# A macaron layer of two expert blocks around attention: order of the expert weights' loads, of the router's copies, of one normalisation's statistics, and a second area for split shared weights

## The reference

```python
def layernorm(x): return (x - mean(x)) / sqrt(var(x) + 1e-5)

def ffn(x2, gate_w, w_gate_up, w_down, sh_gate_up, sh_down):     # 1024 tokens of 512
    g_s, u_s = split(x2 @ sh_gate_up.T)                          # shared: inner width 512
    shared = silu(g_s) * u_s @ sh_down.T
    probs = softmax(x2 @ gate_w.T)                               # 16 experts
    top_w, top_i = top_k(probs, 2); top_w /= top_w.sum()
    out_e = (silu(x2 @ gate_e.T) * (x2 @ up_e.T)) @ down_e.T     # expert: inner width 128
    return sum(top_w * out_e over the 2 chosen) + shared

x = x + 0.5 * ffn(layernorm(x), ...)
x = x + attention(layernorm(x))        # causal, 2 x 512 tokens, 32 heads on 8 key/value heads of 128
x = x + 0.5 * ffn(layernorm(x), ...)   # same weights again
```

## Time and profile before

| | us |
|---|---|
| median of 3 runs | 1133.6 |
| lowest, highest | 1132.75, 1134.34 |
| the profiled execution's own time | 1136.42 |
| its span in the profile | 1134.4 |
| PE busy | 1092.4 (96%) |
| DVE busy | 798.8 (70%) |
| ACT busy | 640.2 (56%) |
| POOL busy | 541.7 (48%) |

### The profile page before, as it was taken

One profiled execution on the slowest core, in us unless ns is written; L12 is line 12 of the kernel. 1 busy time (PEld: TensorE's weight loads), 2 busy tenths in 40 slices (PEclk: granted clock), 3 DMA queues, 4 the chain that ended last, 5 costly groups with the idle time before them and its releaser, 6 DMA issues.

```text
span 1134.4 us, 22421 instructions
## 1 busy us (share of the span) xinstructions
PE 1092.4 (96%) x6584; PEld 943.7 (83%) x6584; DVE 798.8 (70%) x2139; ACT 640.2 (56%) x1737; POOL 541.7 (48%) x540
## 2 busy tenths in 40 slices
PE   8979999899999999999999999999999998989997
PEld 6867877688988988998898898898899986777875
DVE  7857868766766667667676676666766777668866
ACT  4347753466656556646555665655665655357750
POOL 1545647165337336426526533733642540456644
PEclk9989999999999999999999999999999999999999
DMA  9995665100200200110110020020010005955546
GB/s 355 409 347 189 189 213 191 49 1 1 94 2 1 93 0 0 48 44 0 37 55 0 0 92 0 0 92 0 0 37 1 1 2 191 385 203 168 186 164 208
DMA packets 38622, 114.85 MB, mean 101 GB/s; under 512 B 4384, under 2 KB 4384, under 8 KB 36512
## 3 DMA queue, kind: packets, MB, share of 16 engines
q1 hardware_dynamic: 33440, 97.30, 23.8%
q0 software_dynamic: 5120, 16.78, 4.3%
HBM read 79.20 MB, written 34.87 MB: 101 GB/s over the span
## 4 chain that ended last, share of the span: by engine, by line
PE 80%; DVE 6%; DMA 4%; ACT 4%; POOL 3%; issue 3%; SPq 0%; DVEq 0%; POOLq 0%; ACTq 0%
PE bank L1610 22%; PE bank L1649 13%; PE bank L1741 9%; PE bank L1682 9%; PE bank L1585 7%; PE bank L1623 6%; PE bank L1596 4%; PE bank L1499 2%; PE bank L1546 2%; DMA xn<-x_rows 2%; POOL yg L593 1%; POOL x_rows L582 1%; PE bank L1518 1%; PE bank L1737 1%; PE bank L1678 1%
## 5 line engine op out<-in xcount | busy, mean ns | idle before, releaser
L611 POOL TENSOR_TENSOR scores<-scores,pinv 128x512 f32<-128x512 f32 (+3 forms) x256 | 180.2, 736 | 205.4 <-DVE pinv L1317 205.4
L1216 DVE TENSOR_TENSOR pT_lo<-bank,pT_hi 128x512 fp32r<-128x512 f32 (+2 forms) x192 | 101.0, 554 | 92.9 <-ACT pT_hi L849 92.7
L554 POOL TENSOR_TENSOR tback_lo<-experts,tback_hi 128x768 fp32r<-128x768 f32 x62 | 114.0, 1840 | 65.9 <-ACT tback_hi L756 65.7
L878 ACT ACTIVATE scores<-scores,nmax 128x512 f32<-128x512 f32 (+3 forms) x256 | 140.6, 561 | 0.0
L1281 DVE CUSTOM_DVE_ANT_0 scores<-bank,causal 128x512 f32<-128x512 f32 (+3 forms) x256 | 112.2, 486 | 1.4 <-issue 0.4
L849 ACT ACTIVATE pT_hi<-bank 128x512 fp32r<-128x512 f32 (+2 forms) x192 | 87.0, 489 | 41.6 <-PE bank L1623 41.5
L1610 PE MATMUL bank<-xnT_hi,wqs_hi 128*128 128x512 f32 x256 | 102.8, 402 | 0.6 <-DVE vv_lo L1220 0.6
L1610 PE MATMUL bank<-xnT_lo,wqs_hi 128*128 128x512 f32 x256 | 101.4, 396 | 0.0
L1610 PE MATMUL bank<-xnT_hi,wqs_lo 128*128 128x512 f32 x256 | 101.3, 396 | 0.0
L1623 PE MATMUL bank<-ident,scores 128*128 128x128 f32 x640 | 91.1, 273 | 2.8 <-DVE pT_lo L1216 2.4
L1623 PEld LDWEIGHTS bank<-ident,scores 128*128 128x128 f32 x640 | 75.6, 141 | 11.8 <-DVE pT_lo L1216 2.6
(11 more groups left out here) (242 smaller groups left out, 3516.5 us busy)
## 6 DMA issues: line engine op xcount, KB each, us to landing
experts<-in_ffn_w SPq DMA_DIRECT2D x32, 768.0 KB, 11.4
xn<-x_rows SPq DMA_DIRECT2D x62, 256.0 KB, 2.8
y_rows<-xn SPq DMA_DIRECT2D x62, 256.0 KB, 2.0
raw_q<-in_wq SPq DMA_DIRECT2D x8, 1024.0 KB, 5.4
raw_d<-in_wd SPq DMA_DIRECT2D x8, 1024.0 KB, 4.8
x_rows<-experts SPq DMA_DIRECT2D x1, 7936.0 KB, 30.7
raw_w<-in_ffn_w SPq DMA_DIRECT2D x8, 768.0 KB, 6.5
raw_kv<-in_wkv SPq DMA_DIRECT2D x8, 512.0 KB, 3.5
```

Of the source, the lines that this page charges most:

```text
L554: nc.gpsimd.tensor_tensor(tback[par][1][:], experts[:, bass.ds(at + FRONT, GU - FRONT)], tback[par][0][:].bitcast(F32), ALU.subtract).then ...
L611: nc.gpsimd.tensor_tensor(s, s, pinv[k % 2][:, i:i + 1].to_broadcast([P, P * (i + 1)]), ALU.mult).then_inc(att.normed, 1)
L878: nc.scalar.activation(s, s, ACT.Exp, bias=nmax[par][:, i:i + 1], scale=-1.0, accum_out=psumr[par][:, i:i + 1]).then_inc(att.exp, 1)
L1216: nc.vector.tensor_tensor(pT[1][:, lo_col:hi_col], bank[b][:, 0:hi_col - lo_col], pT[0][:, lo_col:hi_col].bitcast(F32), ALU.subtract).then ...
```

## The change

Four edits go together.

1. **Experts' loads.** The experts come in quarters of four. For `n = 0` only experts 0 to 5 are issued ahead of the scatter's wait (4 and 5 after the first quarter has landed); 6 and 7 follow the loads of tiles 0 to 3; 8 to 11 follow those of tiles 4 and 5 and a wait for the second quarter; 12 follows the store of tile 2 and waits for the third quarter; 13, and 14 with 15, stand between loads and stores of tiles 8 to 10. For `n = 1` experts 4 to 7 wait until the first quarter has landed, 8 to 11 until two have, 12 to 15 until three have. Expert 13 (`HELD_BACK`) waits besides for `u_mm >= 4`, slot 3's up product, in either block. ACT's waits count in quarters, in both blocks, up to step 9; after that all 16 are awaited.
2. **Second pair of areas.** `wgu_odd` holds the odd quarters of the shared gate/up weights. It lies over the experts' area (from 20 x 1024 numbers on, which is in experts 13 and 14); so `cut_gu(3)` waits until all tiles are done. `cut_gu` now stands ahead of `gate` in ACT's list, and `low_gu` ahead of `multiply` in DVE's.
3. **Router.** The first half's logits are copied ahead of `gate(0)`, the second half's behind it; `high(0)` follows. DVE's `low(0)` moves behind the router's first part.
4. **Statistics and adds.** Of `statistics(2, 0)`, the BN_STATS of tiles 2 and 3 move to the end of the slot ahead (`statistics_ahead`), the rest behind the three `turned_lo` of the last slot; the chain of small steps after it (`scaled`) moves into the last slot, and ACT's `roots` behind its last `turned_hi`. In each block's end half of `combine(n, 0)` moves behind `multiply` of slot 6. At the kernel's end `add_down` of slot 7 is divided: two tiles' adds stand ahead of `combine(1, 6)`.

```diff
-EARLY_TILES = 7
-LOADED_HALF = NEXP // 2 * 16
+EARLY_TILES = 9
+QUARTER = NEXP // 4
+LOADED_QUARTER = QUARTER * 16
+LOADED_ALL = NEXP * 16
+WGU_AT = 20 * GU
+HELD_BACK = WGU_AT // FW
...
+        def gate_weights(e):
+
+            return wgu_odd if e % 2 else wgu
+
...
+            quarter = LOADED_QUARTER * (QUARTER - 1)
+            early = [(word >> 4 * (k - 1) if k else word << 4) & quarter for k in range(RING + 2)]
+            return at, [e + LOADED_QUARTER for e in early]
...
                 def load_expert(e):
+                    if e == HELD_BACK:
+
+                        sp.wait_ge(ffn[n].u_mm, 4)
                     sp.dma_start(experts[:, e * FW:(e + 1) * FW], ffn_w[e]).then_inc(moe[n].weights, 16)
...
+                def quarters_there(count):
+
+                    sp.wait_ge(moe[n].weights, count * LOADED_QUARTER)
+
+                def load_quarter(q):
+                    for e in range(QUARTER * q, QUARTER * q + QUARTER):
+                        load_expert(e)
+
+                load_quarter(0)
                 if n == 1:
-                    load_shared(n, 2)
-
-                sp.wait_ge(moe[n].weights, LOADED_HALF)
+                    quarters_there(1)
+                    load_quarter(1)
+                load_shared(n, 2)
                 if n == 0:
...
+                    quarters_there(1)
+                else:
+                    for q in (2, 3):
+                        quarters_there(q)
+                        load_quarter(q)
...
+                def some(experts_at):
+                    if n == 0:
+                        for e in experts_at:
+                            load_expert(e)
...
+                some((4, 5))
                 sp.wait_ge(route[n].scattered, 2 * TT * 16)
                 for k in range(4):
                     load_tile(n, 0, k)
...
+                some((6, 7))
                 load_tile(n, 1, 0)
...
                 load_tile(n, 1, 1)
-                for e in left[3:]:
-                    load_expert(e)
+                if n == 0:
+                    quarters_there(2)
+                some((8, 9, 10, 11))
                 for k in range(4):
                     store_tile(n, 0, k)
                     if k < 2:
                         load_tile(n, 1, k + 2)
-                with sp.Fori(2, TILES // 4) as it:
+                    if n == 0 and k == 2:
+                        sp.wait_ge(once.cleared, 16)
+                        quarters_there(3)
+                        some((12,))
+                for k in range(4):
+                    load_tile(n, 2, k)
+                    some(((13,), (14, 15), (), ())[k])
+                    store_tile(n, 1, k)
...
-                wait(act, f.u_mm, 2 * e)
-                nc.scalar.activation(wgu[0][:].rearrange("p c k i -> p (c k i)"), raw_w[e % 2][:, 0:GU],
+                wait(act, f.u_mm, 2 * (e - 1))
+                if e == NSH - 1:
+
+                    act.wait_ge(moe[n].y_mm, TILES)
+                nc.scalar.activation(gate_weights(e)[0][:].rearrange("p c k i -> p (c k i)"), raw_w[e % 2][:, 0:GU],
...
-                        back(1 - par, at[k + 2], there[k + 2] if n == 0 and j < EARLY_TILES else 2 * LOADED_HALF)
+                        back(1 - par, at[k + 2], there[k + 2] if j < EARLY_TILES else LOADED_ALL)
...
-                shared(n, 0, 1)
-                router(n)
+                router(n, 0)
+                gate(n, 0)
+                router(n, 1)
+                high(n, 0)
...
-                combine(n, 0)
+                combine(n, 0, (0,))
                 multiply(n, SLOTS - 2)
+                combine(n, 0, (1,))
                 low(n, SLOTS - 2)
...
+            add_down(1, SLOTS - 1, range(0, HALF // 2))
             combine(1, 6)
-            add_down(1, SLOTS - 1)
+            add_down(1, SLOTS - 1, range(HALF // 2, HALF))
```

83 lines of the change are left out of this document (42 added, 41 removed).

## The result

| | us |
|---|---|
| changed kernel, median of 10 runs | 1138.26 (1135.23 to 1141.82) |
| kernel before, median of 10 runs on the same chip | 1134.21 (1132.40 to 1138.09) |
| ratio, 95% interval | 1.0031 (1.0016 to 1.0046) |
| changed kernel, span of the profiled execution (its time 1137.25) | 1135.4 |
| PE busy | 1096.7 (97%) |

The change costs 0.3%, some 4 us. Forecast were 1126.5 us and a gain of 7; the result lies outside the range, on the other side.

A forecast was written before the change was run, and what follows sets the result against it. PE, busy 96% of the span, was taken as the bound, so only its waits could gain. -4.9 - 0.3 - 0.7 - 1.15 = -7.05 us from 1133.6 gave 1126.5 us, range 1121.5 to 1130.5.

The forecast's parts named there:

- Step 1, the scatter: First block: with fewer expert loads beside it, the scatter lands at 60.9 for 63.66 us, -2.8 us.
- Step 1, the clock: First block, after the scatter: a shorter PE wait means less loss at half rate, -0.5 us.
- Step 1, tile 6: First block: the tile's load lands at 81.6, before PE asks at 82.1; its wait goes, -1.8 us.
- Step 1, tile 10: First block: the load behind experts 14 and 15 lands within half a us of its need, +0.2 us.
- Rival A: First block: experts queued ahead delay loads of tiles 6, 8 and 10; kernel slower by 3.1 us, 1136.7; chance 0.05.
- Step 2, second areas: Splitting of shared gate/up weights only changes place and hides; price 0, between -0.2 and +1.1 us.
- Step 3, router: Router: earlier first logits copy saves PE's 0.67 us wait; worth -0.66 us ahead of the second block's scatter.
- step 4, end of attention: End of attention: moved statistics remove PE's 2.44 us wait, but later waits take most back; -0.95 us.
- Step 5, the second scatter: Second block: experts 13 to 15 beside the scatter give back 1.6 us; -0.3 us together with router and end of attention.
- The sign that was named for this: Forecast is wrong if SP's waits for quarters leave the DMA engines idle longer than 2 us each.
- rival C: Second block: scatter lands 6.69 us after its last issue and low clock follows, +2 us; 1128.7; chance 0.13.
- Step 6, ends: Block ends: moved multiply gives -0.7 us in the first, two adds moved ahead give -1.15 in the second.

The follow-up runs named there:

- e8: Changed kernel with late experts issued behind tiles' loads in both blocks and stores behind loads; 1135.66 us, 0.9867 of before, where before takes some 1151 us.
- e9: e8 with the first block's loads and stores put back as in the changed kernel; 0.9971 of before, where before takes some 1135 us.
- e11: e8 without the second pair of areas and with no expert held back; 1127.72 us, 0.9929 of before, where before takes some 1135 us.
- e5: The kernel before, unchanged, traced as a control on a chip of the slower kind, where it takes some 1151 to 1152 us.
- e16: Kernel before with only the second pair of areas and the second block's loads by quarters; 1.0057 of before, where before takes some 1135 us.

## Why the prediction was wrong, point by point

**Step 1, the scatter: right, and too small.** Forecast -2.8 us, landed at 60.9; it landed at 58.32, and PE's first tile came 5.3 us earlier. Of the 2.6 us between, 1.6 are the time from last issue to landing, 4.3 us forecast from the second block, 2.72 measured, and 2.7 in e8 and e9 too (994.67 to 997.40; 995.31 to 998.04). The 4.3 were not free of loads, as the step said: SP's loads had ended by some 994, but the scatter's own backlog kept the engines full until 998. The other 1.0 us is the last issue, at 55.59 and not 56.6: POOL started 0.8 us earlier instead of 0.35, and its sixteen pieces took 20.3 us in place of 20.9. The Trainium skill, page "DMA: Bandwidth & Descriptors", section "Anatomy of one DMA — SWDGE (gpsimd) path", gives about 2.0 us of fixed cost and the bytes on top; 2.7 for 256 KB agrees with that.

**Step 1, the clock: -0.5 forecast, no gain measured.** PE's first wait was 0.38 us and not 3.0. But the 1.46 us wait behind it, which was to stay, grew to 1.94, and the half rate came there, until 71.4. From the first tile's row until PE asks for tile 6 it is 19.0 us in both traces.

**Step 1, tile 6: right by luck.** The forecast had the row at 82.1 without a wait; it stands at 81.93 with a wait of 1.82. Two errors cancel. PE asked at 80.1, 2 us earlier than forecast, since the scatter had landed earlier. The load landed at 81.88 for 81.6, 23.6 us behind the scatter's landing instead of 20.7: four experts were to take 7.7 us behind SP's wait, yet from 68.39, when eight had landed, tile 6's load took until 81.9, since tiles' loads and stores run beside (4.5 MB in all, where four experts are 3.15).

**Step 1, tile 10: the failed step.** "+0.2", because the load "lands within half a us of its need". It took 8.22 us, issued 2.4 us behind experts 14 and 15 and not 5; tile 10 waits 2.68 us and ACT 2.21, and the low clock comes with it: +5.6 us between tile 6 and tile 12 where +0.2 stood. Tiles were asked for from PE's side and the queue was a check at the end. From the scatter on it is the queue that sets the time: ten experts stand behind it in place of seven, and from its landing at 58.3 until the last expert's at 96.3 the queue moves 12.7 MB with the DMA engines 92% busy. What PE had won at the first tile became waiting at a later one. Rival A had this mechanism, with waits of 1.8, 3.4 and 5.2 us for the 1.8, 0.3 and 2.7 measured, and got a chance of 0.05. e11 bears it out from the other side: the same early scatter, no wait, and 5.2 us less at the block's last tile than e9.

**Step 2, second areas "price 0".** Right for what it looked at: PE never waited for the split weights on chips at 1135. On chips at 1151 it does, 5.10 us in e5, which the trace of the forecast couldn't show.

**Step 3, router, and step 4, end of attention: right.** Forecast -1.6 ahead of the second scatter; the router's row is 1.7 us earlier, 0.4 of it from the first block, and the 0.67 us wait for the logits behind it is gone too. The 2.08 us wait is the "some 2 us for `left_a_lo`"; the further 1 us ahead of the transposes didn't come, so the end of attention gave 1.3 us for 0.95. The scatter's last issue is 2.7 us earlier instead of 1.6; the granted clock of the router's stretch, which step 5 left open, rose to 1.00.

**Step 5, the second scatter: right mechanism, wrong size, and the second step that failed.** Forecast: last issue 995.35, landed at 1001.6, PE at 1004.2 after 2.7, another 1.0 by the clock, price -0.3 for steps 3 to 5. Measured: 994.22, 1002.67, 1005.19 after 5.84, and 2.3 by the clock. Against before, tile 0's first product is 2.8 us later, though attention began 0.4 us earlier: +3.2 for -0.3. PE was free at 999.4 and not at 1001.5, and the landing took 8.4 us from the last issue and not 6.25. The missed term is the waits for quarters: the sum let only 13 to 15 be late, by the hold, from 991.8 on, and gave the quarters nothing. In the trace the hold costs SP 0.7 us and the quarters 20.9; 12 to 15 all start behind 988.5, and from 990 to 996 the scatter's queue moves 0.11 MB per us, not 0.16. The sign that was named for this, DMA engines idle for over 2 us at a quarter's wait, is there: a share of 0.13 from 960 to 964. The forecast's side estimate for three such waits, 6 us of transfer time, was of the right size (3.0 MB at 0.41 MB per us are some 7 us) and stayed out of the sum. Two sums of the forecast are also out by a little: 7 us from 993.8 is 1000.8 and not 1001.6, and rival C's terms give 1128.9 and not 1128.7. Alone this part costs 6.5 us (e16). Rival C had a loss at this scatter, priced at +2 for steps 3 to 5.

**Step 6, ends: right.** -1.15 forecast, -1.2 measured at the kernel's end. In the first block `down(6)` no longer waits, and PE's transposes start at 190.67 for 191.19 (forecast -0.7; tile 12 was 0.3 us late), but at half rate, 3.53 us for 2.03:

```profile
190.67 3.53 PE L1482 MATMUL bank<-ident,xn 128*128 128x128 f32 x16 [1.96 <-DVE xn L1063]
...
209.15 2.02 PE L1482 MATMUL bank<-ident,xn 128*128 128x128 f32 x16 [0.47 <-DVE xn L1063]
```

The second row stood at 209.54 before, behind a wait of 1.68 us. That wait takes up most of what the half rate cost, and PE enters attention 0.4 us earlier.

**The sum.** -4.9 for the first block's loads became +0.3 at tile 12, -0.3 for steps 3 to 5 became +3.2, the rest came in. The chances gave 0.05 to slower, and the range ended at 1130.5. Both errors have one shape: PE came about 2 us earlier than forecast (tile 6, second scatter), and the transfers it then waited for did not.

## What to carry to other kernels

When an early transfer is bought by putting others behind it, add up what the queue must move from that point on and compare it with when each consumer asks; a gain at the first consumer is only kept if the last one's data also come earlier. Put weights behind the first tiles' loads, one per tile, and let the engine that uses them wait for groups, not for all; with the small moves that gave 0.7% (chip at 1135) to 1.3% (at 1151). Count what a wait of the issuing engine keeps out of the queue: in the changed kernel's trace the waits for quarters moved four experts' bytes from ahead of the scatter to beside its end. Price a long wait of PE with the half rate behind it, not with the wait alone: 1.7 us behind 2.68, 2.3 behind 5.84 here.
